# Stores of the MLP stage: one transfer for a block of 512 tokens in place of four for its tiles of 128

## The chip, the cores and the metric

The kernel runs on one core of one Trainium2 chip. The metric is the device time of one execution in microseconds (us), median of three runs. Two timings of this kernel that differ by under 0.2% can't be told apart.

## What is computed

One layer of a graph network over 6250 tokens (nodes) of 512 features, in float32:

```python
xn = layernorm(x)
x  = x + gnn(xn) + mix(xn)           # gnn: xn + relu([xn, mean of the edges' attributes] @ W1 + b1) @ W2 + b2
x1n = layernorm(x)                   # x is "x1" in the kernel
probs  = softmax(mean(x1n, tokens) @ Wg + bg)     # one choice for all tokens
expert = argmax(probs)
x  = x + probs[expert] * (x1n @ We[expert] + be[expert])
```

The stage that the change is in computes `x1` and `x1n` from what earlier stages left in HBM. The last line is the next stage.

## The kernel before

The kernel is a sequence of stages, each a block of five instruction streams, one for each engine, that synchronise by semaphores. All engines meet between two stages. The stage of the change (`gnn_stage`) is called the MLP stage here; the stage behind it (`expert_stage`) reads `x1` and `x1n` back from HBM and can't begin before the MLP stage's stores have landed.

Tokens are taken in blocks of BT = 512: twelve whole blocks (b = 0 to 11) and a tail block (b = 12) of 106. A block has CH = 4 tiles (s = 0 to 3) of P = 128 tokens. The order of the work is written out by hand in each engine's stream. Products in float32 are done as three float32r products of high and low halves.

For each block:

- **SP** loads ahead. It issues the five edge tables of block b + 3 when VectorE has added those of b + 2, then `pre` of b + 2 (2048 KB), then, when `x1_ready` counts the last tile of b, `base` of b + 2 (1024 KB).
- **TensorE (PE)**: `hidden` makes the hidden layer of block b + 1, eight slices of two matmuls, between the outputs of block b. `output(b, s)` is 24 matmuls into one of two `acc` banks and waits until VectorE has emptied that bank (`x1_ready`). `turn_x1(b, s)` transposes the normalised rows of a tile, and stands in the stream one output later: output 1, turn 0, hidden, output 2, turn 1, hidden, output 3, turn 2, output 0 of the next block, turn 3. Behind turn 0 stands one more transpose, of the tables' means.
- **VectorE (DVE)**, per tile: `first_half` adds `acc` and `base` to `x1[s % 2]` (L1897), then bn_stats and bn_aggr; `add_pre` and `low` serve the hidden layer; `second_half` takes the reciprocal and writes `x1n` (L1911). At the end of a block stands `add_tables`.
- **ScalarE (ACT)**, per tile: `deviation1` takes the square root; `rectify` serves the hidden layer; `turned` copies the transposed tile from PSUM to `x1nT[s % 2]` in four pieces (L1815), one tile later.
- **GpSimd (POOL)**, per tile: `store_x1` stores `x1[s % 2]`, waits until that transfer has landed and only then counts `x1_free` up; `store_x1nT` does the same with `x1nT[s % 2]` and `x1nT_free`. They alternate, x1 of tile s and then x1nT of tile s - 1, in one stream.

So `first_half` waits for `x1_free` before it writes a tile into the buffer of the tile two before, and `turned` for `x1nT_free`. A tile of x1 is stored as 128 rows of 2 KB; a tile of x1nT as 512 pieces of 128 tokens, 512 bytes each.

Of the kernel before, what the change touches and what calls it, by code (L numbers as in the profile page):

```python
# [5 lines left out]
ALU = mybir.AluOpType  # L6
# [7 lines left out]
P = 128  # L14
TOKENS = 6250
DIM = 512
# [1599 lines left out]
def gnn_stage(nc, c):  # L1616


    with ExitStack() as ctx:
# [24 lines left out]
        pre = [sb(f"pre{k}", [P, JH, BT]) for k in range(2)]  # L1644
        base = [sb(f"base{k}", [P, CH, DIM]) for k in range(2)]
        hid = [sb(f"hid{k}", [P, BT]) for k in range(2)]
        x1 = [sb(f"x1_{k}", [P, DIM]) for k in range(2)]
        raw1, mv1, std1, rstd1 = sb("raw1", [P, 6]), sb("mv1", [P, 2]), sb("std1", [P, 1]), sb("rstd1", [P, 1])
        x1n = sb("x1n", [P, DIM])
        x1nT = [sb(f"x1nT{k}", [P, CH, P]) for k in range(2)]  # L1650
        part = [sb(f"part{k}", [P, CH]) for k in range(2)]
        turn_bank = [bank(f"turn{k}") for k in range(2)]
        agg_bank = bank("agg_bank")
# [14 lines left out]
        table_in, agg_step = sem("table_in"), sem("agg_step")  # L1668
        agg_turned, agg_hi_ready, agg_ready = sem("agg_turned"), sem("agg_hi_ready"), sem("agg_ready")
        h_mm, hid_ready, h_hi_ready, h_ready = sem("h_mm"), sem("hid_ready"), sem("h_hi_ready"), sem("h_ready")  # L1670
        acc_mm, x1_ready, x1_stored, x1_free = sem("acc_mm"), sem("x1_ready"), sem("x1_stored"), sem("x1_free")
        raw1_ready, mv1_ready, std1_ready, rstd1_ready = sem("raw1_ready"), sem("mv1_ready"), sem("std1_ready"), sem("rstd1_ready")
        x1n_ready, x1n_turned, x1nT_ready = sem("x1n_ready"), sem("x1n_turned"), sem("x1nT_ready")
        x1nT_free, x1nT_stored, parts_added = sem("x1nT_free"), sem("x1nT_stored"), sem("parts_added")
        block = ctx.enter_context(nc.Block())

        @block.sync
# [109 lines left out]
        def _(act):  # L1787
# [20 lines left out]
            def turned(b, n, s):  # L1808

                r = subtiles(n)[s]  # L1810
                act.wait_ge(x1n_turned, b * CH + (s + 1))
                act.wait_ge(x1nT_free, b * CH + s + 1)
                act.wait_ge(parts_added, b * CH + s)
                for ch in range(CH):
                    op = act.activation(x1nT[s % 2][:, ch, 0:r], turn_bank[s % 2][:, ch * P:ch * P + r], ACT.Copy,  # L1815
                                        accum_out=part[s % 2][:, ch:ch + 1])
                op.then_inc(x1nT_ready, 1)

# [26 lines left out]
        def _(dve):  # L1845
# [43 lines left out]
            def first_half(b, k, n, s):  # L1889

                r = subtiles(n)[s]
                at = b * CH + (s + 1)
                if s == 0:
                    dve.wait_ge(base_in[k], landed(b, k, 2))
                dve.wait_ge(acc_mm, at)
                dve.wait_ge(x1_free, b * CH + s + 1)
                dve.tensor_tensor(x1[s % 2][0:r, :], acc[s % 2][0:r, :], base[k][0:r, s, :], ALU.add  # L1897
                                  ).then_inc(x1_ready, 1)
                dve.wait_ge(x1_ready, at + AHEAD)
                dve.bn_stats(raw1[0:r, :], x1[s % 2][0:r, :]).then_inc(raw1_ready, 1)  # L1900
                dve.wait_ge(raw1_ready, at)
                dve.bn_aggr(mv1[0:r, :], raw1[0:r, :]).then_inc(mv1_ready, 1)

            def second_half(b, n, s):
                r = subtiles(n)[s]
                at = b * CH + (s + 1)
                dve.wait_ge(std1_ready, at)
                dve.reciprocal(rstd1[0:r, :], std1[0:r, :]).then_inc(rstd1_ready, 1)
                dve.wait_ge(rstd1_ready, at)
                dve.wait_ge(x1n_turned, b * CH + s)  # L1910
                dve.tensor_scalar(x1n[0:r, :], x1[s % 2][0:r, :], mv1[0:r, 0:1], rstd1[0:r, :],  # L1911
                                  ALU.subtract, ALU.mult).then_inc(x1n_ready, 1)

            def add_part(b, s):
# [53 lines left out]

        @block.gpsimd
        def _(pool):  # L1970
            pool.sem_inc(x1_free, AHEAD)
            pool.sem_inc(x1nT_free, AHEAD)

            def store_x1(b, n, s):
                r = subtiles(n)[s]
                pool.wait_ge(x1_ready, b * CH + (AHEAD + s + 1))
                pool.dma_start(c.x1[bass.ds(b * BT + s * P, r), :], x1[s % 2][0:r, :]).then_inc(x1_stored, 16)  # L1977
                pool.wait_ge(x1_stored, b * (16 * CH) + 16 * (s + 1))
                pool.sem_inc(x1_free, 1)

            def store_x1nT(b, n, s):
                r = subtiles(n)[s]
                pool.wait_ge(x1nT_ready, b * CH + (AHEAD + s + 1))
                pool.dma_start(c.x1n[:, bass.ds(b * BT + s * P, r)].rearrange("(c p) t -> p c t", p=P),  # L1984
                               x1nT[s % 2][:, :, 0:r]).then_inc(x1nT_stored, 16)
                pool.wait_ge(x1nT_stored, b * (16 * CH) + 16 * (s + 1))
                pool.sem_inc(x1nT_free, 1)

            def body(b, k, n, after):
                ns = len(subtiles(n))  # L1990
                for s in range(ns):
                    store_x1(b, n, s)
                    if s >= 1:
                        store_x1nT(b, n, s - 1)
                store_x1nT(b, n, ns - 1)

            all_blocks(pool, 2, body)


LATE = ("gate_step", "gate_mm", "gate_exp", "gathered", "w_hi_ready", "w_ready", "x_in0", "x_in1", "x_in2",  # L2000
        "x_in3", "x1_in0", "x1_in1", "x1_in2", "x1_in3", "xT_hi_ready", "xT_ready", "y_mm", "y_ready",
# [296 lines left out]
```

## Time and profile before

| | us |
|---|---|
| median of 3 runs (2339.5 to 2341.2) | 2339.61 |
| the profiled execution's own time | 2349.22 |
| its span in the trace | 2347.5 |
| MLP stage, first to last x1 tile written | 1748.17 to 2158.75 |
| first load of the next stage | 2180.82 |
| TensorE busy | 1947.9 (83% of the span) |
| VectorE busy | 1221.4 (52%) |
| ScalarE busy | 562.2 (24%) |
| GpSimd busy | 1381.0 (59%) |

Busy shares are means over stages with different limits, so they tell little of this stage. What counts is what TensorE does there, which of its waits ends last, and what the wait was for. GpSimd's busy time in the MLP stage is only the issuing of its stores.

### The profile page before, as it was taken

To read this page: it belongs to the slowest core of one execution; us is meant where nothing else is said; L and a number is where in the kernel's file an instruction comes from. 1 tells how busy PE (TensorE), PEld (TensorE's weight loads), DVE (VectorE), ACT (ScalarE), POOL (GpSimd) and SP (SyncE) were. 2 spreads that over 40 slices of the span, in tenths; PEclk is the share of its full clock that TensorE was granted. 3 is DMA by queue.
4 is the path that set the end of the run, shared out by engine and by line. 5 is a ranking of instruction groups with operands and counts; after the bars stand their busy time and mean duration, and the time that the engine had idled before them with its cause. 6 is when DMAs were issued, how large, how long until landed. Compare 5 with 4: busy or idle time off the path is not lost. (4 is left out here: it accounts for less than half of the span.)

```text
span 2347.5 us, 31355 instructions
## 1 busy us (share of the span) xinstructions
PE 1947.9 (83%) x10775; PEld 1535.1 (65%) x10775; DVE 1221.4 (52%) x3855; ACT 562.2 (24%) x1314; POOL 1381.0 (59%) x948
## 2 busy tenths in 40 slices
PE   1899999999999997887378777777749898897598
PEld 1688888887888885443167666666637676675486
DVE  3533434544443342766356565645467666663475
ACT  1322223322222321111212212111123323332110
POOL 3688888888888886776568878878701111111100
PEclk9999999999999997667678888867869999998799
DMA  9677777877877777988879999998566465542684
GB/s 274 161 153 149 148 126 156 151 151 144 161 145 129 141 139 172 228 194 220 184 160 188 181 191 160 189 181 158 76 194 201 156 184 157 160 145 75 219 310 157
DMA packets 517818, 397.47 MB, mean 169 GB/s; under 512 B 349179, under 2 KB 386315, under 8 KB 517662
## 3 DMA queue, kind: packets, MB, share of 16 engines
q1 hardware_dynamic: 389870, 340.90, 51.4%
q0 software_dynamic: 127792, 54.60, 23.2%
q8 instruction: 85, 1.39, 0.2%
q14 instruction: 71, 0.58, 0.1%
HBM read 242.42 MB, written 152.96 MB: 168 GB/s over the span
## 5 line engine op out<-in xcount | busy, mean ns | idle before, releaser
L272 POOL DMA_INDIRECT table<-edge_sums,edge_row x831 | 1304.9, 1570 | 385.0 <-issue 262.9
L218 DVE SCALAR_TENSOR_TENSOR edge_sel<-edge_dst_all,edge_dst_f,upper 128x128 f32<-128x128 int16 x831 | 316.9, 438 | 105.7 <-PE edge_sum L230 96.9
L324 PE MATMUL pr_out_bank<-pr_norm_xT_hi,pr_w_hi 128*128 128x512 f32 (+1 forms) x832 | 329.7, 396 | 0.0
L230 PEld LDWEIGHTS edge_sum<-edge_attr,edge_sel 128*128 128x128 f32 x1662 | 229.9, 209 | 144.6 <-DVE edge_sel L218 114.5
L230 PE MATMUL edge_sum<-edge_attr,edge_sel 128*128 128x65 f32 x1662 | 244.4, 295 | 92.3 <-DVE edge_sel L218 88.3
L324 PE MATMUL pr_out_bank<-pr_norm_xT_lo,pr_w_hi 128*128 128x512 f32 (+1 forms) x832 | 320.6, 385 | 0.0
L324 PE MATMUL pr_out_bank<-pr_norm_xT_hi,pr_w_lo 128*128 128x512 f32 (+1 forms) x832 | 320.4, 385 | 0.0
L240 ACT ACTIVATE edge_sums<-edge_sum 128x260 f32<-128x260 f32 (+1 forms) x209 | 80.7, 386 | 621.4 <-PE edge_sum L230 467.1
L324 PEld LDWEIGHTS pr_out_bank<-pr_norm_xT_lo,pr_w_hi 128*128 128x128 f32 x832 | 156.7, 188 | 33.9
L324 PEld LDWEIGHTS pr_out_bank<-pr_norm_xT_hi,pr_w_lo 128*128 128x128 f32 x832 | 157.1, 189 | 29.6
L324 PEld LDWEIGHTS pr_out_bank<-pr_norm_xT_hi,pr_w_hi 128*128 128x128 f32 x832 | 157.1, 189 | 29.0
L324 PE MATMUL gn_acc<-gn_w_hi,gn_h_hi 128*128 128x512 f32 (+1 forms) x392 | 164.6, 420 | 10.2 <-DVE gn_h_lo L1885 10.0
L1977 POOL DMA_DIRECT2D x_rows<-gn_x x49 | 27.1, 552 | 238.7 <-DMA x1n_T<-gn_x1nT 147.8
L324 PE MATMUL gn_acc<-gn_w_lo,gn_h_hi 128*128 128x512 f32 (+1 forms) x392 | 162.4, 414 | 0.0
L324 PE MATMUL gn_acc<-gn_w_hi,gn_h_lo 128*128 128x512 f32 (+1 forms) x392 | 162.1, 414 | 0.0
L1984 POOL DMA_DIRECT2D x1n_T<-gn_x1nT x49 | 37.2, 759 | 179.0 <-DMA x_rows<-gn_x 128.4
L732 DVE TENSOR_TENSOR pr_stage<-pr_v_bank,pr_bias_v 128x512 f32<-128x512 f32 (+1 forms) x49 | 33.9, 691 | 195.2 <-PE pr_v_bank L324 194.4
L1331 PE MATMUL at_s<-at_q,at_kt 64*128 64x128 f32 (+1 forms) x782 | 100.8, 405 | 29.5 <-ACT at_kt L1411 15.3
L324 PE MATMUL at_acc<-at_wo_hi,at_r_hi 128*128 128x512 f32 (+1 forms) x196 | 91.8, 469 | 36.8 <-DVE at_r_lo L1478 33.3
L691 ACT ACTIVATE pr_stage<-pr_out_bank,bias_qk 128x512 f32<-128x512 f32 (+1 forms) x104 | 68.8, 662 | 215.9 <-PE pr_out_bank L324 196.3
L694 ACT ACTIVATE pr_stage<-pr_out_bank 128x512 f32<-128x512 f32 (+1 forms) x104 | 59.5, 572 | 228.4 <-PE pr_out_bank L324 224.9
L1331 PEld LDWEIGHTS at_s<-at_q,at_kt 64*128 64x128 f32 (+1 forms) x782 | 79.7, 220 | 42.6 <-issue 24.2
(201 smaller groups left out, 3295.7 us busy)
## 6 DMA issues: line engine op xcount, KB each, us to landing
edge_dst_all<-dst SPq DMA_DIRECT2D x103, 256.0 KB
edge_attr<-in_edge_attr SPq DMA_DIRECT2D x103, 256.0 KB
qk_T<-pr_stage SPq DMA_DIRECT2D x48, 512.0 KB
h_pre_T<-pr_stage SPq DMA_DIRECT2D x48, 512.0 KB
gn_pre<-h_pre_T SPq DMA_DIRECT2D x12, 2048.0 KB, 10.5
done<-qk_T SPq DMA_DIRECT2D x16, 1024.0 KB
table<-edge_sums,edge_row POOLq DMA_INDIRECT x831
pr_norm_x<-in_x SPq DMA_DIRECT2D x12, 1024.0 KB
```

The costliest lines, as they stand in the source:

```text
L218: op = dve.scalar_tensor_tensor(out=self.sel[q][0:rows, j, 0:rows], in0=self.dst_all[k][0:rows, t:t + m * (rows - 1) + 1:m], scalar=self.d ...
L230: mm = pe.matmul(self.p_sum[q][0:rows, j * ECOLS:(j + 1) * ECOLS], self.sel[q][0:rows, j, 0:rows], self.attr[k][0:rows, j0 + j, :], start= ...
L240: act.activation(self.sums[k][0:rows, j0:j0 + w, :], self.p_sum[q][0:rows, 0:w * ECOLS] .rearrange("p (w c) -> p w c", w=w), ACT.Copy).the ...
L272: pool.indirect_dma_start(self.c.table[t], bass.IndirectOffsetOnAxis(ap=self.row[k][0:rows, j:j + 1], axis=0), self.sums[k][0:rows, j, :], ...
L324: mm = pe.matmul(out, a, c, start=first and i == 0, stop=last and i == n - 1)
L691: act.activation(pair[p % RING][:, e % 2, 0:n], out_bank[e % 2][:, 0:n], ACT.Sigmoid, bias=c.bias_qk[:, i:i + 1], accum_out=part[k][:, i:i ...
L694: act.activation(pair[p % RING][:, e % 2, 0:n], out_bank[e % 2][:, 0:n], ACT.Copy).then_inc(out_free, 1)
L732: dve.tensor_tensor(v[0:r, i, :], v_bank[i % 2][0:r, :], bias_v[0:r, :], ALU.add).then_inc(v_bank_free, 1)
L1331: mm = pe.matmul(s_bank[half][0:w * HEADS, j * P:j * P + w * HEADS], kt[u][rows, t:t + w, :].rearrange("d t h -> d (t h)"), q[b % 2][rows, ...
L1977: pool.dma_start(c.x1[bass.ds(b * BT + s * P, r), :], x1[s % 2][0:r, :]).then_inc(x1_stored, 16)
L1984: pool.dma_start(c.x1n[:, bass.ds(b * BT + s * P, r)].rearrange("(c p) t -> p c t", p=P), x1nT[s % 2][:, :, 0:r]).then_inc(x1nT_stored, 16)
```

## The change

`x1` and `x1nT` grow from one tile to a whole block, two buffers of each by the block's parity. VectorE and ScalarE write tile s into its part of the block's buffer. GpSimd issues one store of 1024 KB for a block's x1 when all of its tiles are written, and one for its x1nT, and doesn't wait behind them. `x1_free` and `x1nT_free` go; VectorE and ScalarE wait, at the first tile of a block from the third on, until the store of the block two before has landed. The stream of GpSimd is now x1nT of block b - 1, then x1 of block b. At the end of the stage it waits for all stores. A piece of x1nT in HBM is now 2 KB instead of 512 bytes.

```diff
--- before.py
+++ after.py
@@ -1644,10 +1644,10 @@
         pre = [sb(f"pre{k}", [P, JH, BT]) for k in range(2)]
         base = [sb(f"base{k}", [P, CH, DIM]) for k in range(2)]
         hid = [sb(f"hid{k}", [P, BT]) for k in range(2)]
-        x1 = [sb(f"x1_{k}", [P, DIM]) for k in range(2)]
+        x1 = [sb(f"x1_{k}", [P, CH, DIM]) for k in range(2)]
         raw1, mv1, std1, rstd1 = sb("raw1", [P, 6]), sb("mv1", [P, 2]), sb("std1", [P, 1]), sb("rstd1", [P, 1])
         x1n = sb("x1n", [P, DIM])
-        x1nT = [sb(f"x1nT{k}", [P, CH, P]) for k in range(2)]
+        x1nT = [sb(f"x1nT{k}", [P, CH, BT]) for k in range(2)]
         part = [sb(f"part{k}", [P, CH]) for k in range(2)]
         turn_bank = [bank(f"turn{k}") for k in range(2)]
         agg_bank = bank("agg_bank")
@@ -1668,10 +1668,10 @@
         table_in, agg_step = sem("table_in"), sem("agg_step")
         agg_turned, agg_hi_ready, agg_ready = sem("agg_turned"), sem("agg_hi_ready"), sem("agg_ready")
         h_mm, hid_ready, h_hi_ready, h_ready = sem("h_mm"), sem("hid_ready"), sem("h_hi_ready"), sem("h_ready")
-        acc_mm, x1_ready, x1_stored, x1_free = sem("acc_mm"), sem("x1_ready"), sem("x1_stored"), sem("x1_free")
+        acc_mm, x1_ready, x1_stored = sem("acc_mm"), sem("x1_ready"), [sem(f"x1_stored{k}") for k in range(2)]
         raw1_ready, mv1_ready, std1_ready, rstd1_ready = sem("raw1_ready"), sem("mv1_ready"), sem("std1_ready"), sem("rstd1_ready")
         x1n_ready, x1n_turned, x1nT_ready = sem("x1n_ready"), sem("x1n_turned"), sem("x1nT_ready")
-        x1nT_free, x1nT_stored, parts_added = sem("x1nT_free"), sem("x1nT_stored"), sem("parts_added")
+        x1nT_stored, parts_added = [sem(f"x1nT_stored{k}") for k in range(2)], sem("parts_added")
         block = ctx.enter_context(nc.Block())
 
         @block.sync
@@ -1809,10 +1809,11 @@
 
                 r = subtiles(n)[s]
                 act.wait_ge(x1n_turned, b * CH + (s + 1))
-                act.wait_ge(x1nT_free, b * CH + s + 1)
+                if s == 0 and b >= 2:
+                    act.wait_ge(x1nT_stored[b % 2], b // 2 * 16)
                 act.wait_ge(parts_added, b * CH + s)
                 for ch in range(CH):
-                    op = act.activation(x1nT[s % 2][:, ch, 0:r], turn_bank[s % 2][:, ch * P:ch * P + r], ACT.Copy,
+                    op = act.activation(x1nT[b % 2][:, ch, s * P:s * P + r], turn_bank[s % 2][:, ch * P:ch * P + r], ACT.Copy,
                                         accum_out=part[s % 2][:, ch:ch + 1])
                 op.then_inc(x1nT_ready, 1)
 
@@ -1893,11 +1894,12 @@
                 if s == 0:
                     dve.wait_ge(base_in[k], landed(b, k, 2))
                 dve.wait_ge(acc_mm, at)
-                dve.wait_ge(x1_free, b * CH + s + 1)
-                dve.tensor_tensor(x1[s % 2][0:r, :], acc[s % 2][0:r, :], base[k][0:r, s, :], ALU.add
+                if s == 0 and b >= 2:
+                    dve.wait_ge(x1_stored[b % 2], b // 2 * 16)
+                dve.tensor_tensor(x1[b % 2][0:r, s, :], acc[s % 2][0:r, :], base[k][0:r, s, :], ALU.add
                                   ).then_inc(x1_ready, 1)
                 dve.wait_ge(x1_ready, at + AHEAD)
-                dve.bn_stats(raw1[0:r, :], x1[s % 2][0:r, :]).then_inc(raw1_ready, 1)
+                dve.bn_stats(raw1[0:r, :], x1[b % 2][0:r, s, :]).then_inc(raw1_ready, 1)
                 dve.wait_ge(raw1_ready, at)
                 dve.bn_aggr(mv1[0:r, :], raw1[0:r, :]).then_inc(mv1_ready, 1)
 
@@ -1908,7 +1910,7 @@
                 dve.reciprocal(rstd1[0:r, :], std1[0:r, :]).then_inc(rstd1_ready, 1)
                 dve.wait_ge(rstd1_ready, at)
                 dve.wait_ge(x1n_turned, b * CH + s)
-                dve.tensor_scalar(x1n[0:r, :], x1[s % 2][0:r, :], mv1[0:r, 0:1], rstd1[0:r, :],
+                dve.tensor_scalar(x1n[0:r, :], x1[b % 2][0:r, s, :], mv1[0:r, 0:1], rstd1[0:r, :],
                                   ALU.subtract, ALU.mult).then_inc(x1n_ready, 1)
 
             def add_part(b, s):
@@ -1968,34 +1970,31 @@
 
         @block.gpsimd
         def _(pool):
-            pool.sem_inc(x1_free, AHEAD)
-            pool.sem_inc(x1nT_free, AHEAD)
-
-            def store_x1(b, n, s):
-                r = subtiles(n)[s]
-                pool.wait_ge(x1_ready, b * CH + (AHEAD + s + 1))
-                pool.dma_start(c.x1[bass.ds(b * BT + s * P, r), :], x1[s % 2][0:r, :]).then_inc(x1_stored, 16)
-                pool.wait_ge(x1_stored, b * (16 * CH) + 16 * (s + 1))
-                pool.sem_inc(x1_free, 1)
-
-            def store_x1nT(b, n, s):
-                r = subtiles(n)[s]
-                pool.wait_ge(x1nT_ready, b * CH + (AHEAD + s + 1))
-                pool.dma_start(c.x1n[:, bass.ds(b * BT + s * P, r)].rearrange("(c p) t -> p c t", p=P),
-                               x1nT[s % 2][:, :, 0:r]).then_inc(x1nT_stored, 16)
-                pool.wait_ge(x1nT_stored, b * (16 * CH) + 16 * (s + 1))
-                pool.sem_inc(x1nT_free, 1)
+            def store_x1(b, n):
+                r, ns = subtiles(n)[-1], len(subtiles(n))
+                pool.wait_ge(x1_ready, b * CH + (AHEAD + ns))
+                if ns == CH:
+                    pool.dma_start(c.x1[bass.ds(b * BT, n), :].rearrange("(s p) d -> p s d", p=P), x1[b % 2][:, :, :]
+                                   ).then_inc(x1_stored[b % 2], 16)
+                else:
+                    pool.dma_start(c.x1[bass.ds(b * BT, n), :], x1[b % 2][0:r, 0, :]).then_inc(x1_stored[b % 2], 16)
+
+            def store_x1nT(b, n):
+                pool.wait_ge(x1nT_ready, b * CH + (AHEAD + len(subtiles(n))))
+                pool.dma_start(c.x1n[:, bass.ds(b * BT, n)].rearrange("(c p) t -> p c t", p=P),
+                               x1nT[b % 2][:, :, 0:n]).then_inc(x1nT_stored[b % 2], 16)
 
             def body(b, k, n, after):
-                ns = len(subtiles(n))
-                for s in range(ns):
-                    store_x1(b, n, s)
-                    if s >= 1:
-                        store_x1nT(b, n, s - 1)
-                store_x1nT(b, n, ns - 1)
+                if b:
+                    store_x1nT(b - 1, BT)
+                store_x1(b, n)
+                if not after:
+                    store_x1nT(b, n)
 
             all_blocks(pool, 2, body)
-
+            for stored in (x1_stored, x1nT_stored):
+                for k in range(2):
+                    pool.wait_ge(stored[k], 16 * len(range(k, NB, 2)))
 
 LATE = ("gate_step", "gate_mm", "gate_exp", "gathered", "w_hi_ready", "w_ready", "x_in0", "x_in1", "x_in2",
         "x_in3", "x1_in0", "x1_in1", "x1_in2", "x1_in3", "xT_hi_ready", "xT_ready", "y_mm", "y_ready",
```

## Rows read from the trace of the kernel before

**Rows 1.** Busy time by window: us, (instructions), then granted clock, DMA share, GB/s.

```profile
1759.80:1788.10 28.30, 28.17 (x132) 22.87 (x132) 23.82 (x46) 10.85 (x45) 3.94 (x6) 1.00 0.78 238
1788.10:2136.90 348.80, 307.29 (x1334) 242.78 (x1333) 229.70 (x446) 108.35 (x450) 51.51 (x79) 0.94 0.50 155
2158.00:2181.00 23.00, 2.06 (x11) 1.31 (x9) 2.72 (x8) 2.66 (x18) 4.19 (x6) 0.57 0.21 64
2217.00:2337.00 120.00, 119.92 (x529) 98.80 (x528) 86.30 (x104) 17.83 (x10) 0.00 (x0) 1.00 0.71 246
```

**Rows 2.** Waits in 1710 to 2200 us: total us, times, longest.

```profile
POOL x_rows L1977 <- DMA x1n_T<-gn_x1nT: 147.8, 36, 7.4
POOL x1n_T L1984 <- DMA x_rows<-gn_x: 128.4, 35, 6.4
DVE gn_x L1897 <- POOLq L1979: 90.4, 26, 5.9
...
PE gn_turn L1741 <- DVE gn_x1n L1911: 43.3, 18, 3.7
```

**Rows 3.** Timeline of GpSimd, successive stores in a middle block.

```profile
1963.57 0.54 POOL L1977 DMA_DIRECT2D x_rows<-gn_x  x1 [7.38 <-DMA x1n_T<-gn_x1nT]
1966.90 0.76 POOL L1984 DMA_DIRECT2D x1n_T<-gn_x1nT  x1 [2.79 <-DMA x_rows<-gn_x]
1970.85 0.76 POOL L1984 DMA_DIRECT2D x1n_T<-gn_x1nT  x1 [3.18 <-DMA x1n_T<-gn_x1nT]
```

**Rows 4.** Timeline of VectorE: start and duration of five writes of an x1 tile.

```profile
1759.84 0.68 DVE L1897 TENSOR_TENSOR gn_x<-gn_acc,gn_base 128x512 f32<-128x512 f32 x1
...
1788.08 0.69 DVE L1897 TENSOR_TENSOR gn_x<-gn_acc,gn_base 128x512 f32<-128x512 f32 x1 [0.30 <-PE gn_acc L324]
...
1966.45 0.69 DVE L1897 TENSOR_TENSOR gn_x<-gn_acc,gn_base 128x512 f32<-128x512 f32 x1 [4.96 <-POOLq L1979]
...
2136.90 0.69 DVE L1897 TENSOR_TENSOR gn_x<-gn_acc,gn_base 128x512 f32<-128x512 f32 x1 [2.86 <-POOLq L1979]
...
2158.75 0.69 DVE L1897 TENSOR_TENSOR gn_x<-gn_acc,gn_base 106x512 f32<-106x512 f32 x1 [2.50 <-PE gn_acc L324]
```

**Rows 5.** Timeline of TensorE in one block.

```profile
1953.83 0.60 PE L1741 MATMUL gn_turn<-ident,gn_x1n 128*128 128x128 f32 x4
1954.19 0.48 PE L1750 MATMUL gn_h<-gn_agg,gn_w_hi 128*128 128x512 f32 x1
...
1971.54 0.40 PE L324 MATMUL gn_acc<-gn_w_hi,gn_h_hi 128*128 128x512 f32 x1
...
1976.90 0.40 PE L324 MATMUL gn_acc<-gn_w_lo,gn_h_hi 128*128 128x512 f32 x1
```

**Rows 6.** Timeline of all engines at the end of the MLP stage.

```profile
2161.55 0.97 PE L1741 MATMUL gn_turn<-ident,gn_x1n 106*128 106x106 f32 x4 [2.46 <-DVE gn_x1n L1911]
...
2168.30 0.26 ACT L1815 ACTIVATE gn_x1nT<-gn_turn 128x106 f32<-128x106 f32 x1 [5.41 <-issue]
...
2177.01 0.79 POOL L1984 DMA_DIRECT2D x1n_T<-gn_x1nT  x1 [3.75 <-issue]
2180.82 0.38 SPq L2050 DMA_DIRECT2D ex_xT<-x1n_T  x1
```

**Rows 7.** Timeline of SP's queue: loading of the tables in a middle block.

```profile
1952.56 2.56 SPq L1693 DMA_DIRECT2D gn_agg_raw<-table  x5
```

**Rows 8.** DMA issues over the span: count, KB each, median us to landing.

```profile
gn_pre<-h_pre_T SPq DMA_DIRECT2D x12, 2048.0 KB, 10.5
...
gn_base<-base_rows SPq DMA_DIRECT2D x12, 1024.0 KB, 6.6
x_rows<-gn_x POOLq DMA_DIRECT2D x48, 256.0 KB, 2.3
x1n_T<-gn_x1nT POOLq DMA_DIRECT2D x48, 256.0 KB, 3.5
...
gn_agg_raw<-table SPq DMA_DIRECT2D x60, 130.0 KB
```

## The prediction

> **What bounds the kernel now.** I read the busy time by window first, because the means over the whole span mix stages. The last 120 us are TensorE's: busy 119.92 of 120.00 us at a granted clock of 1.00. The MLP stage is not like that. From 1788.10 to 2136.90 us TensorE is busy 307.29 of 348.80 us, its granted clock is 0.94, and the DMA engines are busy for half of the time. No engine is full there. Yet in the same stage, from 1759.80 to 1788.10, TensorE is busy 28.17 of 28.30 us at a clock of 1.00 [rows 1].
>
> Next the waits, to see what holds TensorE. Its largest wait in the stage is in front of the transposes, 43.3 us, for `x1n` from VectorE. VectorE in its turn waits 90.4 us in 26 places before it writes a tile of x1, for GpSimd's count `x1_free`. And GpSimd's own time goes into waiting for its own stores: 147.8 us for an x1nT to land before it can issue an x1, and 128.4 us the other way round [rows 2]. GpSimd's timeline shows one link: an x1nT issued at 1966.90 is followed by the next issue at 1970.85, 0.76 us of issuing and 3.18 us of waiting [rows 3].
>
> So the bound of the stage is a serial chain of eight stores a block. By the medians an x1 takes 0.54 us of issue and 2.3 to land, and an x1nT 0.76 and 3.5 [rows 3, 8]: 4 x (2.84 + 4.26) = 28.4 us a block before any wait for data. Each store also can't start before its tile is ready, and each tile can't be written before a store two back has landed. The loop of the two comes out longer than either. VectorE's write at 1966.45 shows it: it stood 4.96 us for the count while its operands were there [rows 4].
>
> **The size of the loop.** A block's second tile of x1 is written at 1788.08 in block 1 and at 2136.90 in block 11: ten block periods in 348.82 us, 34.88 each. The same tile of block 0 is at 1759.84, so the first period was 28.24 us [rows 4]. In that one no store had to be waited for, and it is the window in which TensorE was full [rows 1]. I take it as TensorE's floor, and check it by counting: four outputs of 24 matmuls, at (1976.90 - 1971.54) / 23 = 0.233 us each, are 22.4 us; 16 matmuls of the hidden layer at the same pace are 3.7; five groups of transposes at 1954.19 - 1953.83 = 0.36 us or a little more are 1.9 [rows 5]. The sum is 28.0, against 28.24 measured.
>
> **The change part by part.**
>
> *Waits behind each store, removed.* GpSimd no longer stands behind a transfer. VectorE's wait for x1 is now for a store issued at the end of the block two before. Between that issue and the need lies about one block, 28 us. For the price of a 1024 KB store I have bounds: a 256 KB one lands in 2.3 or 3.5 us, so four of them in 9.2 or 14; a 1024 KB load, `base`, lands in 6.6 [rows 8]. All are far below 28, so the new wait costs nothing; the work that hides it is a whole block of TensorE. If this cover went, VectorE's in-order stream would stop at the first tile, with `add_pre` of the next block and then TensorE's hidden layer behind it. ScalarE's wait is the same with x1nT, a tile later.
>
> *What is late next.* VectorE was busy 23.82 us in the 28.30 us window [rows 1], so it has 4.5 us to spare in a block at TensorE's pace; small gaps between its instructions will take about half of that. ScalarE has 17 us to spare. Hence TensorE is next, and the period falls from 34.88 to about 28.3 (the count above gives 28.0, the measured one 28.24). The ten periods give 10 x 6.58 = 65.8 us. Part of it is idle time of TensorE, and part is clock: the granted 0.94 returns to 1.00 when the gaps are gone, as it was in the first period.
>
> *Blocks 11 and 12.* From tile 1 of block 11 to the tail's tile takes 21.85 us now [rows 4]. TensorE's work there is three outputs (16.8), three groups of transposes (1.1) and the tail's five hidden slices, of 106 columns, some 1.3: 19.2. That gives 2.7 us.
>
> *The end of the stage.* The tail's tile is written at 2158.75 [rows 4] and the next stage's first load is at 2180.82 [rows 6], 22.07 us later, because GpSimd is several stores behind. In the new kernel only the real chain stands there. The transposes begin 2.80 us after the tile and take 0.97; ScalarE's four copies, 0.27 each with their accumulator reads, some 1.1, end at 4.9; then the last store takes 2180.82 - 2177.01 = 3.8 us from its issue to the next stage [rows 6], so 8.8 us at the best. But block 11's x1nT, 1024 KB, is issued only some 2 us ahead of it and shares the engines. With 6.6 us for such a transfer [rows 8] from an issue at about +3.5 the end comes at 10 to 11. I take 11 and a gain of 11.1; bounds 8.8 and 17.5 (14 us for the store), a gain of 13.3 to 4.6.
>
> The Trainium skill ("DMA: Bandwidth & Descriptors", SECNAME) says a DMA costs about 2.0 us fixed plus its bytes at 436 GB/s. The 2.3 us of a 256 KB x1 store [rows 8] agree. By that rule the 1024 KB store would land in some 4.4 us, and the sum would be about 2 us lower.
>
> *Descriptors and issue.* 98 issues of GpSimd become 26, the larger ones at 0.76 us or a little more; GpSimd is on nobody's path then. The pieces of x1nT grow from 512 bytes to 2 KB: fewer packets, no loss.
>
> *Everything else* (the stages before, 1748 us of them, and the 167 us from 2180.82 on) is unchanged: 0.
>
> The sum is 65.8 + 2.7 + 11.1 = 79.6 us. The profiled execution's span of 2347.5 becomes 2268, its own time of 2349.22 becomes 2270, and since the median of the runs is 9.6 us below that, the median becomes 2260.
>
> **The rivals.**
>
> *A. Partly given back (period 29 to 31.5).* VectorE's stream is in order and 84% full in the fast window. At the end of a block it has `add_tables` beside the shortest of TensorE's intervals, and delays there could pass on to TensorE; each also lowers the clock for a moment. For it: the stage has only one period of proof, with loads already issued. Against it: that proof contained an `add_tables` too. At 30 us a period the gain is 48.8 + 2.7 + 11 = 62, a time of 2277.
>
> *B. The burst of transfers becomes the bound.* Both x1's store and the load of `base` start when a block's fourth tile is written, the tables (1952.56, in five issues, [rows 7]) and `pre` some 5 to 8 us behind, and x1nT just after. A block moves 2.10 + 1.05 + 0.67 + 2.10 = 5.9 MB [rows 8]. At a period of 28.3 us that is 209 GB/s, where the fast window carried 238 and the last stage 246 [rows 1]. The tables of the next block must land within about a period. It decides from the point where the mix runs below 209 GB/s: at 188 the period is 31.4 and the time 2291; the sign turns only below 169 GB/s (5.9 / 34.88), which gives **slower than before**, at 160 GB/s 36.9 us a period, 20 us lost, less 14 for the last blocks and the end: 2346. For it: the stores have never come as 1024 KB from this queue. Against it: the rates above. The Trainium skill (same page, "Issuing engines are not separate DMA queues") says that GpSimd's and SP's transfers share the same 16 engines and interleave, which is this rival's ground; no row shows it decide.
>
> *C. The stores were hidden anyway.* Then the change does nothing: 2339. VectorE's 90.4 us of waits [rows 2] overlap others, but TensorE's idle time and clock are real, and the first period is 6.6 us shorter than the rest; I see no other releaser that would step in at 34.9.
>
> **How the numbers follow.** The forecast (period 28.0 to 29.0, end 9 to 17 us) has 0.66, with a range of its own from 2254 to 2273. A has 0.21, and the milder part of B, up to 2300, 0.06. A gain smaller than that has 0.03, C 0.02, slower 0.02. Nine in ten should lie from 2250 to 2292: below, the floor of 28.0 a period (3 us less) and the best end (2 us) with some margin; above, 31.5 us a period. Faster by over 0.2% (4.7 us) has 0.96, same 0.02, slower 0.02.
>
> **What would show it.** The profile after should have no wait of VectorE for GpSimd at L1897's successor; second tiles 28.3 us apart; TensorE busy over 98% at a clock of 1.00 from 1790 to some 2070 us; the first load of the next stage at about 2101. The prediction is wrong if a DMA (tables, `pre`) appears as releaser on VectorE, if the transposes still wait for `x1n`, or if the 1024 KB stores take over 25 us to land.

## The result and the profile after

The changed kernel takes 2263.28 us (median of 4 runs, 2260.96 to 2265.66) against 2340.40 for the kernel before (4 runs): a ratio of 0.967, 95% interval 0.9653 to 0.9687, 77.1 us less. The forecast was 2260, with a range from 2250 to 2292. The profiled execution has a span of 2259.2 us.

The busy time by window shows the stage from block 0's second tile to block 1's, from there to block 11's, and its end (the columns are those of [rows 1]):

```profile
1751.60:1779.90 28.30, 28.16 (x131) 22.92 (x132) 23.82 (x46) 10.85 (x45) 0.89 (x1) 1.00 0.73 212
1779.80:2061.70 281.90, 281.90 (x1320) 229.60 (x1318) 230.15 (x446) 107.02 (x451) 15.85 (x21) 1.00 0.61 194
2081.00:2094.00 13.00, 1.35 (x8) 0.79 (x6) 2.62 (x8) 2.45 (x18) 2.13 (x3) 0.61 0.34 114
```

TensorE is busy 281.90 of 281.90 us at a granted clock of 1.00, where it had 307.29 of 348.80 at 0.94 [rows 1]. VectorE is busy 82% of the time, the DMA engines 61%. The end of the stage is shorter but still holds almost no work. The waits of the stage:

```profile
POOL x_rows L1977 <- DVE gn_x L1899: 245.7, 12, 82.8
...
POOL x1n_T L1984 <- ACT gn_x1nT L1816: 137.1, 13, 12.0
...
DVE gn_x L1899 <- PE gn_acc L324: 41.5, 28, 4.1
...
PE gn_turn L1741 <- DVE gn_x1n L1913: 2.5, 1, 2.5
```

No engine waits for GpSimd any more; GpSimd waits for data. VectorE's 41.5 us are for TensorE. The 43.3 us that TensorE stood in front of the transposes [rows 2] are 2.5 us, once. GpSimd's timeline in a middle block, to be held against [rows 3]:

```profile
1808.42 0.75 POOL L1984 DMA_DIRECT2D x1n_T<-gn_x1nT  x1 [12.01 <-ACT gn_x1nT L1816]
1823.94 0.75 POOL L1977 DMA_DIRECT2D x_rows<-gn_x  x1 [14.77 <-DVE gn_x L1899]
1836.71 0.75 POOL L1984 DMA_DIRECT2D x1n_T<-gn_x1nT  x1 [12.01 <-ACT gn_x1nT L1816]
```

One store of each kind a block, 28.29 us apart, each with idle time before it that ends with its data. The tiles of [rows 4]:

```profile
1751.60 0.68 DVE L1899 TENSOR_TENSOR gn_x<-gn_acc,gn_base 128x512 f32<-128x512 f32 x1
...
1779.84 0.69 DVE L1899 TENSOR_TENSOR gn_x<-gn_acc,gn_base 128x512 f32<-128x512 f32 x1 [0.30 <-PE gn_acc L324]
...
2061.70 0.69 DVE L1899 TENSOR_TENSOR gn_x<-gn_acc,gn_base 128x512 f32<-128x512 f32 x1 [2.64 <-PE gn_acc L324]
...
2081.04 0.69 DVE L1899 TENSOR_TENSOR gn_x<-gn_acc,gn_base 106x512 f32<-106x512 f32 x1 [2.97 <-PE gn_acc L324]
```

The first period is 28.24 us as before. The ten that follow take 281.86 us, 28.19 each, where they took 34.88 [rows 4]. The stretch from block 11's second tile to the tail's is 19.34 us, where it was 21.85. The end of the stage, as in [rows 6]:

```profile
2083.84 0.97 PE L1741 MATMUL gn_turn<-ident,gn_x1n 106*128 106x106 f32 x4 [2.46 <-DVE gn_x1n L1913]
...
2084.33 0.75 POOL L1984 DMA_DIRECT2D x1n_T<-gn_x1nT  x1 [7.71 <-ACT gn_x1nT L1816]
...
2085.70 0.22 ACT L1816 ACTIVATION_READ_ACCUMULATOR gn_x1nT<-gn_turn 128x1 f32 x1
...
2086.21 0.79 POOL L1984 DMA_DIRECT2D x1n_T<-gn_x1nT  x1 [0.54 <-ACT gn_x1nT L1816]
2093.92 0.38 SPq L2049 DMA_DIRECT2D ex_xT<-x1n_T  x1
```

From the tail's tile to the next stage's first load it is 2093.92 - 2081.04 = 12.88 us, where it was 22.07. The last store's issue comes 5.17 us after the tile, but the next stage starts 7.71 us behind it, not 3.81 as in [rows 6]; a0, e7 and e8 below take this apart. The landings, in the columns of [rows 8]:

```profile
gn_base<-base_rows SPq DMA_DIRECT2D x12, 1024.0 KB, 6.6
x_rows<-gn_x POOLq DMA_DIRECT2D x12, 1024.0 KB, 9.2
x1n_T<-gn_x1nT POOLq DMA_DIRECT2D x12, 1024.0 KB, 8.1
```

**Where the time went, in the two traces.** The ten periods 66.96 us, the last blocks 2.51, the end 9.19, the rest of the kernel 1.40: 80.06 us from block 0's second tile to the end of the span (587.66 before, 507.60 after). The spans differ by 88.3; the other 8.24 lie ahead of that tile, in code that the change doesn't touch. In the eleven more traces below that tile lies anywhere from 1755.5 to 1766.2 us, the latest in the second trace of the unchanged kernel. So that part is variation between executions, and the comparison of traces is best made from that tile on. One table for all of them (us):

| kernel | second tile of block 0 | mean of the ten periods | last blocks | end of stage | tile to end of span |
|---|---|---|---|---|---|
| before | 1759.84 | 34.88 | 21.85 | 22.07 | 587.66 |
| b0_unchanged | 1766.24 | 34.82 | 21.61 | 22.17 | 584.96 |
| changed | 1751.60 | 28.19 | 19.34 | 12.88 | 507.60 |
| a0_changed | 1762.75 | 28.19 | 19.35 | 12.88 | 507.75 |
| e1_tiles_no_wait | 1760.98 | 28.19 | 19.35 | 10.67 | 505.72 |
| e2_deep_wait | 1764.95 | 30.47 | 23.29 | 59.87 | 580.95 |
| e3_x1_only | 1758.28 | 28.19 | 19.34 | 14.27 | 509.82 |
| e4_x1nT_only | 1765.27 | 28.19 | 19.34 | 16.07 | 512.53 |
| e5_one_x1_buffer | 1762.04 | 29.62 | 18.53 | 13.23 | 525.36 |
| e6_twice | 1755.54 | 28.19 | 19.34 | 15.78 | 511.66 |
| e7_last_by_tile | 1757.64 | 28.19 | 19.34 | 11.40 | 506.86 |
| e8_two_tiles_no_wait | 1762.07 | 28.19 | 19.34 | 9.49 | 504.53 |
| e9_long_pieces | 1763.10 | 30.94 | 19.34 | 22.12 | 545.80 |

### The profile page after: what moved, and what is told of

The parts are those of the page before. It is cut to its first block and busy times, and to the rows that moved or that the text cites. A ratio compares the mean times of both kernels' runs of the same rounds, so it can differ in the third digit from the quotient of the medians.

```text
span 2259.2 us, 31150 instructions
## 1 busy us (share of the span) xinstructions
PE 1923.5 (85%) x10775; PEld 1529.0 (68%) x10775; DVE 1221.2 (54%) x3855; ACT 560.9 (25%) x1314; POOL 1339.2 (59%) x876
## 5 line engine op out<-in xcount | busy, mean ns | idle before, releaser
L230 PEld LDWEIGHTS edge_sum<-edge_attr,edge_sel 128*128 128x128 f32 x1662 | 237.9, 215 | 139.9 <-DVE edge_sel L218 106.8
L230 PE MATMUL edge_sum<-edge_attr,edge_sel 128*128 128x65 f32 x1662 | 252.6, 301 | 88.7 <-DVE edge_sel L218 83.9
L324 PE MATMUL gn_acc<-gn_w_hi,gn_h_hi 128*128 128x512 f32 (+1 forms) x392 | 156.2, 399 | 6.3 <-DVE gn_h_lo L1886 6.3
L324 PE MATMUL gn_acc<-gn_w_lo,gn_h_hi 128*128 128x512 f32 (+1 forms) x392 | 156.7, 400 | 0.0
L324 PE MATMUL gn_acc<-gn_w_hi,gn_h_lo 128*128 128x512 f32 (+1 forms) x392 | 155.4, 396 | 0.0
L1977 POOL DMA_DIRECT2D x_rows<-gn_x x12 | 9.2, 764 | 245.7 <-DVE gn_x L1899 245.7
L324 PE MATMUL at_acc<-at_wo_hi,at_r_hi 128*128 128x512 f32 (+1 forms) x196 | 88.3, 450 | 26.8 <-DVE at_r_lo L1478 26.8
L447 DVE TENSOR_TENSOR pr_norm_xT_lo<-pr_turn,pr_norm_xT_hi 128x512 fp32r<-128x512 f32 (+1 forms) x49 | 33.8, 690 | 136.5 <-ACT pr_norm_xT_hi L441 121.7
```

The costliest lines, as they stand in the source:

```text
L230: mm = pe.matmul(self.p_sum[q][0:rows, j * ECOLS:(j + 1) * ECOLS], self.sel[q][0:rows, j, 0:rows], self.attr[k][0:rows, j0 + j, :], start= ...
L324: mm = pe.matmul(out, a, c, start=first and i == 0, stop=last and i == n - 1)
L447: dve.tensor_tensor(lo, bank, hi.bitcast(F32), ALU.subtract).then_inc(self.split[s % len(self.split)], 1)
L1977: pool.dma_start(c.x1[bass.ds(b * BT, n), :].rearrange("(s p) d -> p s d", p=P), x1[b % 2][:, :, :]).then_inc(x1_stored[b % 2], 16)
```

## The experiments

The kernels were run in four sets, each on one chip with runs of the kernel before beside them; that kernel's median was 2345.20, 2349.28, 2330.48 and 2348.75 us in the four. Ratios are to the kernel before in the same set.

### e1: no waits behind the stores, nothing gathered

The changed kernel's buffers, but a store for each tile.

```diff
-            def store_x1(b, n):
+            def store_x1(b, n, s):
+                r = subtiles(n)[s]
+                pool.wait_ge(x1_ready, b * CH + (AHEAD + s + 1))
+                pool.dma_start(c.x1[bass.ds(b * BT + s * P, r), :], x1[b % 2][0:r, s, :]).then_inc(x1_stored[b % 2], 16)
...
-                    dve.wait_ge(x1_stored[b % 2], b // 2 * 16)
+                    dve.wait_ge(x1_stored[b % 2], b // 2 * (16 * CH))
```

> Two block buffers of each kind as in the changed kernel, but stores by tile (eight a block, pieces of 512 bytes for x1nT), and GpSimd waits behind none of them. Theory (the serial waits behind the stores were the bound): block period 28.3 us as in the changed kernel, and at the end of the stage no 1024 KB store ahead of the last, so 9 to 11 us there; 2259 to 2264 us. Rival (the gathering itself did it: fewer transfers, longer pieces): little of the gain, period 32 to 35, 2305 to 2340 us.

2270.93 us, ratio 0.9691 (0.9652 to 0.9729). By the table the period is the same 28.19 and the end 2.2 us shorter. Busy time by window:

```profile
1790.00:2070.00 280.00, 280.00 (x1307) 227.92 (x1306) 229.38 (x445) 106.99 (x450) 52.20 (x81) 1.00 0.62 193
```

TensorE is as full as in the changed kernel, with eight stores a block and x1nT in pieces of 512 bytes. The gathering is not what made the change fast; the theory holds and its rival falls. The run's median is above the 2264 that I had as the upper end, though its stage is the shorter one: the difference is the part ahead of the stage, 9.4 us later in its trace than in the changed kernel's.

### e2: deeper buffers, the waits kept

```diff
-        x1 = [sb(f"x1_{k}", [P, DIM]) for k in range(2)]
+        x1 = [sb(f"x1_{k}", [P, CH, DIM]) for k in range(2)]
...
-            pool.sem_inc(x1_free, AHEAD)
-            pool.sem_inc(x1nT_free, AHEAD)
+            pool.sem_inc(x1_free, 2 * CH)
+            pool.sem_inc(x1nT_free, 2 * CH)
```

> The kernel before with buffers for eight tiles of each kind, GpSimd still waiting behind every store. Theory: the serial chain alone is 4 x (2.84 + 4.26) = 28.4 us a block by the medians, so deeper buffers break the loop but not the chain: period 28.4 to 30, GpSimd busy or waiting for landings all the time, and the end of the stage 15 to 22 us; 2268 to 2290 us. Rival (depth is irrelevant, the chain's throughput was the whole bound): period stays at 34.9, 2340 us. Rival (depth is everything): as fast as the changed kernel, 2260 to 2264 us.

2344.81 us, ratio 0.9992 (0.9973 to 1.0011): no difference. My expectation of 2268 to 2290 was wrong, and its first rival (depth is irrelevant) was right in the time of 2340. It was not right in the period: that stays at 28.29 us for the first five, goes up to 37.7 behind them and has a mean of 30.47, and the rest of the time stands at the end. From the tile on, e2's trace is 6.7 and 4.0 us shorter than the two of the unchanged kernel, which the medians don't show. Busy time by window, in the stage's first part, its second and its end:

```profile
1793.00:1950.00 157.00, 157.00 (x737) 127.98 (x736) 131.61 (x250) 60.80 (x251) 21.65 (x33) 1.00 0.58 186
1950.00:2098.00 148.00, 132.11 (x594) 106.35 (x593) 98.55 (x198) 46.36 (x197) 22.85 (x35) 0.95 0.46 147
2121.00:2181.00 60.00, 0.97 (x4) 0.64 (x4) 2.60 (x7) 2.40 (x17) 11.27 (x17) 0.50 0.22 73
```

The first row is TensorE's full pace, 157.00 of 157.00 us: as long as the buffers aren't full, the blocks run ahead of the stores. In the second VectorE stands for a free buffer, and in the third the stage has nothing left but GpSimd working off its stores for 60 us. The next stage can't start before the last has landed, at 2181.05, where it was 2180.82 [rows 6]. What had been gained in the blocks was given back at the end. GpSimd's waits show why the chain is no shorter:

```profile
POOL x_rows L1977 <- DMA x1n_T<-gn_x1nT: 145.8, 35, 7.5
POOL x1n_T L1984 <- DMA x_rows<-gn_x: 93.4, 31, 6.7
...
POOL x1n_T L1984 <- DMA x1n_T<-gn_x1nT: 51.5, 12, 6.4
...
POOL x_rows L1977 <- DMA x_rows<-gn_x: 28.2, 10, 4.4
```

They sum to 318.9 us; those of the kernel before sum to 340.7 (147.8 and 128.4 in [rows 2], and 64.5 more for x1nT behind x1nT and x1 behind x1). With 98 issues at 0.55 and 0.76 us that was 405 us for 12.25 blocks, 33.1 a block, before any wait for data. Even this is a mean of two parts. In the kernel before, the third and fourth x1nT of a block are issued one behind the other; the fourth of blocks 0 and 10:

```profile
1793.90 0.76 POOL L1984 DMA_DIRECT2D x1n_T<-gn_x1nT  x1 [5.81 <-DMA x1n_T<-gn_x1nT]
...
2141.60 0.76 POOL L1984 DMA_DIRECT2D x1n_T<-gn_x1nT  x1 [3.49 <-DMA x1n_T<-gn_x1nT]
```

Between them GpSimd does nothing but issue and wait for landings, but for one wait of 3.5 us that the profile puts down to VectorE. That is 34.8 us a block, the period itself. In e2, where deeper buffers keep nearly all data ready, the same stores of blocks 9, 10 and 11 are issued after the last large load of SP:

```profile
2114.63 0.76 POOL L1984 DMA_DIRECT2D x1n_T<-gn_x1nT  x1 [3.00 <-DMA x1n_T<-gn_x1nT]
...
2142.31 0.76 POOL L1984 DMA_DIRECT2D x1n_T<-gn_x1nT  x1 [3.24 <-DMA x1n_T<-gn_x1nT]
...
2169.01 0.76 POOL L1984 DMA_DIRECT2D x1n_T<-gn_x1nT  x1 [3.15 <-DMA x1n_T<-gn_x1nT]
```

These are 27.7 and 26.7 us a block, near the 28.4 that the prediction had from medians. From block 0 to block 7, beside SP's loads, e2's chain takes 36.6 us a block (1798.90 to 2055.29). So the medians give the price of the chain without traffic beside it: many stores land in 2.3 and 3.5 us, but beside SP's loads GpSimd waits for one up to 7.5.

### e9: the kernel before with long pieces for x1nT

This kernel changes the order in which the rows of x1n lie in HBM, and the next stage reads them as they lie. It leaves out putting them back in order, so its output is not the layer's, and only its time is compared.

```diff
-                pool.dma_start(c.x1n[:, bass.ds(b * BT + s * P, r)].rearrange("(c p) t -> p c t", p=P),
-                               x1nT[s % 2][:, :, 0:r]).then_inc(x1nT_stored, 16)
+                pool.dma_start(flat[first:first + P * CH * r].rearrange("(p w) -> p w", p=P),
+                               x1nT[s % 2][:, :, :].rearrange("p c t -> p (c t)")[:, 0:CH * r]).then_inc(x1nT_stored, 16)
```

> The kernel before with each x1nT tile stored as 128 pieces of 2 KB in HBM instead of 512 pieces of 512 bytes; the rows of x1n are then laid out in another order, which the next stage reads as they lie. All waits behind stores stay. Theory (the sum of issues and landings of the serial chain is the period): an x1nT store gets as cheap as an x1 store, median 0.55 and 2.3 instead of 0.76 and 3.5, 1.4 us less each, 5.7 a block: period 29 to 30.5, 2285 to 2300 us. Rival (the pieces' size is of no account): 2340 us.

2309.98 us, ratio 0.9817 (0.9775 to 0.986), slower than the 2285 to 2300 expected. The landings:

```profile
x_rows<-gn_x POOLq DMA_DIRECT2D x48, 256.0 KB, 2.3
x1n_T<-gn_x1nT POOLq DMA_DIRECT2D x48, 256.0 KB, 2.3
```

An x1nT store lands in 2.3 us like an x1 store, and the period falls to 30.94, 3.9 us less, where the medians had promised 5.7. The sign and the mechanism hold: shorten the links and the period falls. It also bounds the piece size: worth 3.9 us a block in a serial chain, and nothing once nobody waits (e1, e3, e8). (The end of this kernel is 22.12 us, of which 10.6 lie between the last store's issue at 2131.53 and the next stage. The store itself landed 2.3 us after its issue; the 8.3 us behind that, in which no engine works and nothing is transferred, are not explained. The period is what to compare.)

### e3 and e4: one kind only

e3 gathers x1 alone, e4 x1nT alone; the other kind keeps its tile buffers, its `_free` semaphore and the wait behind each store. The edit of e3:

```diff
             def body(b, k, n, after):
                 ns = len(subtiles(n))
-                for s in range(ns):
-                    store_x1(b, n, s)
-                    if s >= 1:
-                        store_x1nT(b, n, s - 1)
+                for s in range(ns - 1):
+                    store_x1nT(b, n, s)
+                store_x1(b, n)
                 store_x1nT(b, n, ns - 1)
```

> Only x1 gathered by block and not waited for; x1nT as before, by tile, two tile buffers, a wait behind each. Theory: a chain of four x1nT stores is 4 x 4.26 = 17 us, under the 28.3 us of TensorE, so the full gain: period 28.3, 2260 to 2266 us. Rival (each store's waits count in proportion): x1's part of the chain is 2.84 of 7.10, 40% of the gain, about 2308 us.

> Only x1nT gathered by block and not waited for; x1 as before, by tile, two tile buffers, a wait behind each. Theory: four x1 stores are 4 x 2.84 = 11.4 us, under 28.3, so the full gain: period 28.3, 2260 to 2267 us. Rival (in proportion): 60% of the gain, about 2292 us.

e3: 2269.86 us, ratio 0.9672 (0.9641 to 0.9703). e4: 2274.09 us, 0.9683 (0.9647 to 0.9719). Both have the period of 28.19, and an end of the stage 1.4 and 3.2 us longer than the changed kernel's. Both medians lie above their expected ranges, 2260 to 2266 and 2260 to 2267 us, but far from their rivals of 2308 and 2292. The gain doesn't come in proportion. There is a threshold: the chain must be shorter than TensorE's 28.2 us a block, and either half of it already is.

### e5: one buffer for x1

```diff
-        x1 = [sb(f"x1_{k}", [P, CH, DIM]) for k in range(2)]
+        x1 = [sb("x1_0", [P, CH, DIM])] * 2
...
-                if s == 0 and b >= 2:
-                    dve.wait_ge(x1_stored[b % 2], b // 2 * 16)
+                if s == 0 and b >= 1:
+                    dve.wait_ge(x1_stored[(b - 1) % 2], (b - 1) // 2 * 16 + 16)
```

> The changed kernel with one block buffer for x1 instead of two: a block's first tile waits for the store of the block before, which was issued when that block's fourth tile was written, 6.7 us earlier. Theory (only a chain that outruns TensorE costs time): the 1024 KB store takes 0.75 us of issue and some 6.6 to 8 to land, so VectorE waits 1 to 2 us a block, which TensorE has in reserve (VectorE has some 1.7 us of idle time at the tile behind); period 28.3 to 28.8, at most 5 us more than the changed kernel. Rival (the second buffer is what pays): 2 to 5 us a block, 22 to 55 us more.

2287.9 us, ratio 0.9729 (0.969 to 0.9768). From the tile on it takes 17.8 us more than the changed kernel; I had expected at most 5. Waits and landings:

```profile
DVE gn_x L1899 <- DMA x_rows<-gn_x: 46.0, 11, 7.4
...
PE gn_turn L1741 <- DVE gn_x1n L1913: 10.2, 12, 2.5
```

```profile
x_rows<-gn_x POOLq DMA_DIRECT2D x12, 1024.0 KB, 9.2
x1n_T<-gn_x1nT POOLq DMA_DIRECT2D x12, 1024.0 KB, 4.8
```

The wait is the one expected, but 4.2 us a block (46.0 in 11), not 1 to 2, because the x1 store lands in 9.2 us, not 6.6 to 8. TensorE loses 1.4 us of it a block in the ten periods and 3.2 in the first (31.47 us). The second buffer pays, if less than its rival's 22 us. The x1nT store indicates what 1024 KB cost with less beside them: it lands in 4.8 us (median) here, issued 7.3 us behind the load of `pre` (1934.37 and 1941.65 in one block), and in 8.1 in the changed kernel, issued 3.4 us behind it (2003.03 and 2006.44). The changed kernel itself agrees: its x1nT stores at 2034.13 and 2060.08 and its x1 store at 2075.87, with no large load beside them, land in 4.6 us each.

### e6: every store twice

Each whole block's store is issued a second time, to scratch rows (`c.more`) that nobody reads.

```diff
+                    pool.dma_start(c.more[0][bass.ds(b * BT, n), :].rearrange("(s p) d -> p s d", p=P), x1[b % 2][:, :, :]
+                                   ).then_inc(x1_stored[b % 2], 16)
...
+                if n == BT:
+                    pool.dma_start(c.more[1][:, bass.ds(b * BT, n)].rearrange("(c p) t -> p c t", p=P), x1nT[b % 2][:, :, :]
+                                   ).then_inc(x1nT_stored[b % 2], 16)
```

> The changed kernel with every whole block's store issued a second time, to scratch rows of its own that nobody reads: 8.0 MB a block instead of 5.9. Theory (TensorE is the bound and the transfers have room): 8.0 MB in 28.3 us is 283 GB/s, above the 246 that a stage of this kernel has carried and below the 395 of its fullest slices; period 28.3 to 29, up to 5 us more at the end of the stage, 2263 to 2280 us. Rival (the transfers are close to their limit of about 246 GB/s): period 32.5, 2305 us or more.

2268.31 us, ratio 0.9656 (0.9615 to 0.9697), and the period is 28.19:

```profile
1790.00:2070.00 280.00, 280.00 (x1311) 228.11 (x1311) 227.94 (x448) 106.17 (x453) 30.00 (x40) 1.00 0.79 270
```

270 GB/s and a DMA share of 0.79, and TensorE doesn't lose a microsecond. Rival B of the prediction is far off: the changed kernel moves 194 GB/s here. Only the end of the stage is 2.9 us longer.

### a0, e7 and e8: the end of the stage, and the cheapest form of the change

These three ran on one chip. a0 is the changed kernel once more. e7 stores block 11's x1nT by tile. e8 is the kernel before with its two tile buffers, in which VectorE and ScalarE wait for the stores themselves:

```diff
-                dve.wait_ge(x1_free, b * CH + s + 1)
+                if b * CH + s >= 2:
+                    dve.wait_ge(x1_stored[s % 2], (b * CH + s) // 2 * 16)
...
-                pool.dma_start(c.x1[bass.ds(b * BT + s * P, r), :], x1[s % 2][0:r, :]).then_inc(x1_stored, 16)
-                pool.wait_ge(x1_stored, b * (16 * CH) + 16 * (s + 1))
-                pool.sem_inc(x1_free, 1)
+                pool.dma_start(c.x1[bass.ds(b * BT + s * P, r), :], x1[s % 2][0:r, :]).then_inc(x1_stored[s % 2], 16)
```

> The changed kernel once more, on the same chip as the next two. Some 77 us under the kernel before; at the end of the stage 12 to 13 us from the tail's tile to the next stage's first load.

> The changed kernel, but block 11's x1nT stored by tile, so that no 1024 KB store is on its way when the tail's store is issued. In the changed kernel the last store's issue to the next stage took 7.7 us against 3.8 in the kernel before. Theory (the last store shares the engines with the large one): 2 to 4 us less at the end of the stage, period unchanged, so 2 to 4 us (0.1 to 0.2%) under the changed kernel. Rival (the 7.7 us are something else, such as the final waits): no difference.

> The kernel before with its two tile buffers and its stores by tile, but GpSimd waits behind none of them: VectorE and ScalarE wait themselves for the store of the tile two before. Needs no more memory than the kernel before. Theory (the serial waits were all of it): a store of 3 to 7 us fits into the two tiles' time of about 14 us, so the full gain, period 28.3, and a short end of the stage, 9 to 10 us: 0 to 4 us under the changed kernel. Rival (depth is needed too): at least some periods longer, 5 to 30 us over the changed kernel.

a0: 2264.45 us, ratio 0.9716 (0.9698 to 0.9734), which is 66 us under the kernel before in this set and not the 77 expected. e7: 2263.18, 0.9709 (0.969 to 0.9728). e8: 2265.55, 0.9708 (0.9688 to 0.9728). The runs can't tell the three apart. The traces can, from the tile on: e7 takes 0.9 us less than a0, e8 3.2 less. The end of e7 and then of e8 (start, duration):

```profile
2084.97 0.75 POOL L1977 DMA_DIRECT2D x_rows<-gn_x  x1
...
2091.88 0.79 POOL L1984 DMA_DIRECT2D x1n_T<-gn_x1nT  x1 [0.15 <-issue]
2098.50 0.38 SPq L2060 DMA_DIRECT2D ex_xT<-x1n_T  x1
```

```profile
2096.68 0.79 POOL L1981 DMA_DIRECT2D x1n_T<-gn_x1nT  x1 [0.52 <-ACT gn_x1nT L1816]
2101.00 0.38 SPq L2048 DMA_DIRECT2D ex_xT<-x1n_T  x1
```

From the last store's issue to the next stage it is 7.71 us in the changed kernel, 6.62 in e7 and 4.32 in e8, against 3.81 in the kernel before. This stretch has two parts. The first is the store's own landing, counted from its issue; in the order before, changed, e7, e8:

```profile
x1n_T<-gn_x1nT POOLq DMA_DIRECT2D x1, 212.0 KB, 3.3
x1n_T<-gn_x1nT POOLq DMA_DIRECT2D x1, 212.0 KB, 5.0
x1n_T<-gn_x1nT POOLq DMA_DIRECT2D x1, 212.0 KB, 3.6
x1n_T<-gn_x1nT POOLq DMA_DIRECT2D x1, 212.0 KB, 3.1
```

With block 11's large x1nT store beside it the last one lands 1.7 us later than in the kernel before, and e7, which takes that store away, has 1.4 of it back. Block 11's x1, also 1024 KB, plays no part: it has landed before the last store is issued, at 2080.5 in the changed kernel (2075.87 + 4.6) and at 2089.9 in e7 (2084.97 + 4.9). The second part lies between this landing and the next stage: 0.5 us in the kernel before, 2.7 in the changed one, 3.0 in e7 and 1.2 in e8. Busy time by window in that stretch of the changed kernel:

```profile
2091.20:2093.90 2.70, 0.00 (x0) 0.00 (x0) 0.00 (x0) 0.00 (x0) 0.00 (x0) 0.50 0.00 0
```

No engine works and nothing is transferred. So e7's theory holds for 1.4 us, less than the 2 to 4 expected, and its rival (something else, such as the final waits) has the larger part. What it is stays open; the four final waits of GpSimd alone don't give it, since e8 has them too, and e4, with two, has 5.5 us.

e8 says the most. It has the full gain with the memory of the kernel before. The tile buffers were deep enough; it was only GpSimd that must not wait behind its own stores.

### b0: the unchanged kernel again

> The kernel before once more, for a second trace of it: the kernel before has measured 2330 to 2349 us in the last sets of runs, and the changed one 2263 and 2264. Theory (the period before is a sum of landings of transfers, the period after is TensorE's): the second trace shows a period that differs from 34.88 by up to 2 us, while all traces of TensorE-bound variants show 28.19 to 0.01. The first tile of the stage is written between 1739 and 1754 us, with the variation of the stages ahead. Rival (all of the variation is ahead of the stage): period 34.9 again.

2346.76 us, ratio 1.0 (0.998 to 1.0019). The period is 34.82, so here the rival was right: with 34.88 in the first trace, the period before hardly varies between these two. Its first tile, written at 1754.58, is just past the 1754 expected. The tile at 1766.24 is 6.4 us later than in the first trace, 14.6 later than in the changed kernel's. Why the kernel before measured 2330.48 in one set, so that the gain was only 66 us there, was not traced, and the cause stays open.

## Why the prediction held

*What bounds the kernel.* Right in the main point: TensorE idled in this stage for a chain of stores, each waited for. Wrong in how the chain's length came about. The prediction said that 28.4 us of stores a block became 34.9 through the loop with the buffers. e2 cuts that loop and gains nothing, and in the kernel before the chain alone, issues and landings, is 34.8 us a block over ten blocks. The 28.4 was a sum of medians, which fits the chain where SP loads nothing (27.7 and 26.7 in e2) and not beside its loads. It did no harm to the forecast, and that is luck in this one point: the change removed the chain whole, so its length didn't matter. It did harm in e2 and e9, where only a part was removed.

*TensorE's floor.* Right: 28.3 forecast, 28.19 measured, in all eight traces without the full chain and with two buffers (e5, with one, has 29.62). The first period of the old trace, which had no store to wait for, was the new kernel's period to 0.05 us. The ten periods gave 66.96 us for 65.8.

*The clock.* As forecast, granted 1.00 over the whole stretch, where the idle gaps had it at 0.94. It comes with the idle time and was part of the same term.

*Waits on the stores of two blocks before.* Nothing, as forecast. The term behind it was off: a 1024 KB store lands in 9.2 and 8.1 us, not in some 6.6. It lay between the rows that bounded it, 6.6 and 14, and 28 us of cover hid it. From the fit in the Trainium skill ("DMA: Bandwidth & Descriptors", section "Anatomy of one DMA — SWDGE (gpsimd) path"), 2.0 us and the bytes at 436 GB/s, it is estimated at 4.4 us. The trace agrees where the store has little beside it, 4.8 us in e5 and 4.6 in the changed kernel's last blocks, and not beside SP's loads. For 256 KB the same fit gives an estimated 2.6 us, so the 2.3 that the prediction set beside it agree only roughly.

*Blocks 11 and 12.* 2.7 forecast, 2.51 measured.

*The end of the stage.* 11.1 forecast, 9.19 measured: 12.88 us instead of 11. The transfers came out as forecast: block 11's x1nT is issued 3.3 us after the tail's tile and lands in 5.2, and the last store has landed at 10.2. The mis-sized term is what follows the last landing. The prediction took it from the kernel before, 0.5 us inside its 3.8; in the changed kernel it is 2.7, with nothing running, and its cause is open (e7, e8).

*Everything else.* 0 forecast; 1.40 in the two traces, where the stretch from the next stage's first load to the end is 166.68 and 165.28 us. Over all traces it lies between 164.7 and 167.0, so that is variation.

*Rivals.* A (VectorE or the loads give part of it back) didn't occur: VectorE at 82% never made TensorE wait in the ten periods, busy 281.90 of 281.90 us. B (the transfers) is refuted with room, e6. C (hidden anyway) is refuted by the result.

The sum, 79.6 us, came out at 80.06 from the tile on and at 77.1 in the medians.

## What to carry to other kernels

An engine that issues transfers and then waits for each one is a serial resource like any other: add up its issues and landings for a unit of work, and compare with the bounding engine. Add them as totals from the waits, and over the stretch in which the other traffic runs, not as medians: here 34.8 us a block against 28.4. The cheapest cure is to let the engine that needs the buffer do the waiting; gathering and deeper buffers are then matters of the last microseconds, and deeper buffers alone only move the wait to the end.

A gain of this kind has a threshold: as long as the chain is the longer one, each shortening counts (e9, 3.9 us a block), and once it is below the bounding engine's time nothing more comes (half of the chain removed gave all of it, e3 and e4). And a stretch of the old trace in which the wait was absent, here the first block, tells the new pace better than a count of instructions.

## What the runs showed of the hardware

- A 1024 KB store from GpSimd's queue takes 0.75 us to issue, as long as a 256 KB one of 512 pieces (0.76), and lands in 4.6 to 4.8 us with little beside it and in 8.1 to 9.2 (medians) beside SP's loads of 1024 and 2048 KB.
- At 270 GB/s and a DMA share of 0.79 over 280 us, TensorE's pace didn't change by 0.01 us a block.
- A 256 KB store in 128 pieces of 2 KB lands in 2.3 us, in 512 pieces of 512 bytes in 3.5.
- Eight waited stores a block make a chain of 34.8 us beside SP's loads and of 26.7 to 27.7 without them.
- From the last store's landing to the next stage's first load it took 0.5 us in the kernel before, 1.2 in e8, 2.7 in the changed kernel, 5.5 in e4 and 8.3 in e9, with no engine busy; no run shows why.
- TensorE kept a granted clock of 1.00 for 281.90 us without a gap.
